# Doubling the token block of the two feed-forward phases to 512, with one SBUF buffer for the gate and the down weights

## The chip, the cores and the metric

One Trainium2 chip, 8 NeuronCores. Each core runs the same program on one batch element of 8192 tokens; nothing is exchanged between cores. The metric is the device time of the slowest core, in microseconds (us).

## The reference

```python
def ffn(x):                       # x [8, 8192, 1024], weights int32 in -127..127, scale 1/127
    gate = x @ (w_gate/127).T     # [.., 3072]
    up   = x @ (w_up/127).T       # [.., 3072]
    return (silu(gate) * up) @ (w_down/127).T      # [.., 1024]
x = x + 0.5 * ffn(layernorm(x))
x = x + causal_conv(layernorm(x), t)   # FFT over the sequence, filter t of 4096 steps
x = x + 0.5 * ffn(layernorm(x))
```

## The kernel before

All activations are kept transposed, with the 1024 channels as 8 chunks of 128 partitions and the tokens along the free dimension. The program has five stages in a row: the transform of the filter (`p0b`, with the weights cast to bf16 in DRAM beside it), the transposes of the weights (`p0a`), the first feed-forward phase (`ffn_phase("f1")`), the convolution (`p2`), and the second feed-forward phase (`ffn_phase("f3")`). Tiles of the two feed-forward phases carry `f1` or `f3` ahead of their names.

A feed-forward phase first loads the three weight matrices from DRAM into SBUF, each 128 partitions x 24576 bf16 (6144 KB), as `wgT` (gate), `wuT` (up) and `wdT` (down), through the DMA queue of SyncE (SP). They stay there for the whole phase. Then it goes over the tokens in `NBLK` blocks of `SB` = 256, that is 32 blocks. A block i has these steps:

- `prologue(i)`: GpSimd (POOL) issues the load of the block's input into `xsl`; ScalarE (ACT) squares all of it into `lnsl`; TensorE (PE) sums `xsl` and then the squares over the channels with a column of ones (L799 and L804, 8 matmuls each, into `pstat`); VectorE (DVE) makes the layernorm factors from the two rows of sums in about 24 operations on one partition (`rowmath`); SP stores them to DRAM.
- `prologue_b(i)`: POOL loads that row back, broadcast over the 128 partitions (`rbp`), and DVE multiplies it into `lnsl`, 8 operations.
- `gate_up(i)`: for each of the 24 hidden tiles `ht`, 8 gate matmuls (L864) and 8 up matmuls (L879), each with one extra matmul with a single row of weights (L860, L875) that subtracts the mean. ACT applies silu, DVE multiplies by the up result and writes `hid`.
- `down_store(i)`: for each of 8 output tiles, 24 matmuls from `hid` and `wdT` (L916), in PSUM banks that rotate over three; ACT evacuates into `res`, DVE adds the residual from `xsl`, and SP stores `res`. In f1 there follow the sums for the second layernorm (a square of `res` on ACT, L961 and L966 on PE, `row2` on DVE, two stores of a row by SP).

The order of the loop is `gate_up(i)`, `prologue(i+1)`, `prologue_b(i+1)`, `down_store(i)`. Every engine runs its own list strictly in this order; `rec.add` records an operation with the semaphores that it waits for. All ACT and DVE operations are recorded by one helper, so they have the line L83. The load of the next input waits only for its buffer (three `xsl` in f1, two in f3).

Of the kernel before, what the change touches and what calls it, by code (L numbers as in the profile page):

```python
# [6 lines left out]
F32 = mybir.dt.float32  # L7
BF16 = mybir.dt.bfloat16
# [4 lines left out]
SEQ, DIM, HID, KLEN = 8192, 1024, 3072, 4096  # L13
NFFT, P = 16384, 128
SCALE = float(np.float32(1.0 / 127.0))
EPS = 1e-5
SB = 256
NBLK = SEQ // SB
NCH = DIM // P
NHT = HID // P  # L20
# [151 lines left out]
class KB:  # L172
# [569 lines left out]
    def ffn_phase(self, tag):  # L742
        rec = self.rec
        self.mark()
        wgT = self.alloc(tag + "wgT", [P, NCH * HID], BF16)
        wuT = self.alloc(tag + "wuT", [P, NCH * HID], BF16)
        wdT = self.alloc(tag + "wdT", [P, NHT * DIM], BF16)
        nxs = 3 if tag == "f1" else 2
        xsl = [self.alloc(tag + f"xsl{i}", [P, NCH * SB], BF16) for i in range(nxs)]
        lnsl = [self.alloc(tag + f"lnsl{i}", [P, NCH * SB], BF16) for i in (0, 1)]  # L750
        hid = self.alloc(tag + "hid", [P, NHT * SB], BF16)
# [4 lines left out]
        res = self.alloc(tag + "res", [P, NCH * SB], BF16 if tag == "f1" else F32)  # L756
        T = lambda s: tag + s
        f1 = tag == "f1"

        bw = self.barrier_waits()  # L760
        for k, dst in (("g", wgT), ("u", wuT), ("d", wdT)):
            rec.add("sync", lambda sy, k=k, dst=dst: sy.dma_start(
                out=dst[:, :], in_=self.s_wT[k][:, :]),
                waits=[("wThbm", 48)] + bw, incs=[(T("wld" + k), 16)])

        pstat = self.pbank[0]
        pg = [self.pbank[2], self.pbank[3]]
        pu = [self.pbank[4], self.pbank[5]]
        pdn = [self.pbank[6], self.pbf.bitcast(F32), self.pbank[1]]
        xin = (self.xT if f1 else self.s_x2).rearrange("(c p) s -> p c s", p=P)  # L770

        def prologue(i):
            bi = i % 2
            xs = i % nxs
            lw = [("wsumev", 12 if "p0a" in self.phases else 0)]
            if i == 0:
                lw += bw
            if i >= nxs:
                lw.append((T("x1ev"), 8 * (i - nxs + 1)))
            if not f1:  # L780
                lw.append(("x2out", 16 * NGRP if "p2" in self.phases else 0))
            rec.add("gpsimd", lambda gg, i=i, xs=xs: gg.dma_start(
                out=xsl[xs].rearrange("p (c s) -> p c s", c=NCH),
                in_=xin[:, :, i * SB:(i + 1) * SB]),
                waits=[w for w in lw if w[1] > 0], incs=[(T("xld%d" % xs), 16)])
            sqw = [(T("xld%d" % xs), 16 * (i // nxs + 1)), (T("std"), rec.n(T("std")))]
            if i >= 2:
                sqw.append((T("umm"), rec.n(T("umm")) - NHT))
                if f1:
                    sqw.append((T("l2mm"), rec.n(T("l2mm"))))  # L790
            rec.add("scalar", lambda s, bi=bi, xs=xs: s.activation(
                lnsl[bi][:, :], xsl[xs][:, :], AF.Square),
                waits=sqw, incs=[(T("sqd"), 1)])
            stw = [(T("xld%d" % xs), 16 * (i // nxs + 1)), (T("row"), rec.n(T("row"))),
                   ("cst", 32), (T("l2row"), rec.n(T("l2row")))]
            if "p0a" in self.phases:
                stw.append(("wsumev", 12))
            for c in range(NCH):
                rec.add("tensor", lambda t, xs=xs, c=c: t.matmul(  # L799
                    pstat[0:1, 0:SB], self.misc[:, 0:1], xsl[xs][:, c * SB:(c + 1) * SB],  # L800
                    start=(c == 0), stop=(c == NCH - 1)),
                    waits=stw if c == 0 else [])
            for c in range(NCH):
                rec.add("tensor", lambda t, bi=bi, c=c: t.matmul(  # L804
                    pstat[0:1, SB:2 * SB], self.misc[:, 0:1], lnsl[bi][:, c * SB:(c + 1) * SB],
                    start=(c == 0), stop=(c == NCH - 1)),
                    waits=[(T("sqd"), rec.n(T("sqd")))] if c == 0 else [],
                    incs=[(T("std"), 1)] if c == NCH - 1 else ())
            def rowmath(v):
                s_, vv, y, tmp = (rows[0:1, k * SB:(k + 1) * SB] for k in range(4))  # L810
                v.tensor_copy(s_, pstat[0:1, 0:SB])
                v.tensor_mul(tmp, s_, s_)
                v.scalar_tensor_tensor(vv, tmp, -1.0 / DIM, pstat[0:1, SB:2 * SB],
                                       ALU.mult, ALU.add)
                v.tensor_scalar(vv, vv, 1.0, DIM * EPS, ALU.mult, ALU.add)
                v.tensor_single_scalar(y.bitcast(I32), vv.bitcast(I32), 1, ALU.logical_shift_right)
                v.tensor_scalar(y.bitcast(I32), y.bitcast(I32), -1, MAGIC, ALU.mult, ALU.add)
                for _ in range(4):
                    v.tensor_mul(tmp, y, y)
                    v.tensor_mul(tmp, tmp, vv)  # L820
                    v.tensor_scalar(tmp, tmp, -0.5, 1.5, ALU.mult, ALU.add)
                    v.tensor_mul(y, y, tmp)
                v.tensor_scalar(rows_bf[0:1, 0:SB], y, float(np.sqrt(DIM)), None, ALU.mult)
                return v.scalar_tensor_tensor(rows_bf[0:1, SB:2 * SB], s_,
                                              -1.0 / float(np.sqrt(DIM)), y,
                                              ALU.mult, ALU.mult)
            rmw = [(T("std"), rec.n(T("std")))]
            if f1:
                rmw.append(("l2out", rec.n("l2out")))
                if "ln2rows" in self.dbg:  # L830
                    rmw.append(("dbgout", rec.n("dbgout")))
            rec.add("vector", rowmath, waits=rmw, incs=[(T("row"), 1)])
            rec.add("sync", lambda sy, i=i: sy.dma_start(
                out=self.s_rb[tag][i % 2:i % 2 + 1, :], in_=rows_bf[0:1, 0:SB]),
                waits=[(T("row"), rec.n(T("row"))), (T("rbro"), rec.n(T("rbro")) - 16)
                       if rec.n(T("rbro")) >= 32 else (T("row"), rec.n(T("row")))],
                incs=[(T("rbro"), 16)])
# [13 lines left out]
        def gate_up(i):  # L851
            bi = i % 2
            for ht in range(NHT):
                q = ht % 2
                gw = [(T("lnap"), rec.n(T("lnap"))), (T("wldg"), 16)]
                if rec.n(T("silu")) >= 2:
                    gw.append((T("silu"), rec.n(T("silu")) - 1))
                for c in range(NCH):
                    if c == NCH - 1:
# [8 lines left out]
                        waits=gw if c == 0 else [],  # L868
                        incs=[(T("gmm"), 1)] if c == NCH - 1 else ())
# [3 lines left out]
                for c in range(NCH):  # L873
                    if c == NCH - 1:
# [8 lines left out]
                        waits=uw if c == 0 else [],  # L883
# [8 lines left out]
                if i > 0 and ht == 0:  # L892
                    hw.append((T("dmm"), rec.n(T("dmm"))))
                rec.add("vector", lambda v, ht=ht, q=q: v.tensor_mul(
                    hid[:, ht * SB:(ht + 1) * SB], silu[:, q * SB:(q + 1) * SB], pu[q][:, 0:SB]),
                    waits=hw, incs=[(T("hmul"), 1)])

        def down_store(i):
            bi = i % 2
            xs = i % nxs  # L900
            hm = rec.n(T("hmul"))
            for dt in range(NCH):
                pd = pdn[dt % 3]
                dw = []
                if dt == 0:
                    dw = [(T("hmul"), hm), (T("wldd"), 16)]
                    if i > 0:
                        dw.append((("x1out" if f1 else "o_out"), 16 * i))
                    if f1:
                        dw.append((T("l2row"), rec.n(T("l2row"))))  # L910
                    if "x1" in self.dbg and f1:
                        dw.append(("dbgout", rec.n("dbgout")))
                if dt >= 3:
                    dw.append((T("sdev"), rec.n(T("sdev")) - 2))
                for hc in range(NHT):
                    rec.add("tensor", lambda t, dt=dt, hc=hc, pd=pd: t.matmul(  # L916
                        pd[:, 0:SB] if True else None,
# [11 lines left out]
                    xsl[xs][:, dt * SB:(dt + 1) * SB]),  # L929
                    waits=[(T("sdev"), rec.n(T("sdev")))],  # L930
                    incs=[(T("x1ev"), 1)])
            if f1:
                x1o = self.s_x1.rearrange("(c p) s -> p c s", p=P)
                rec.add("sync", lambda sy, i=i: sy.dma_start(
# [17 lines left out]
            if f1:  # L952
# [11 lines left out]
                        waits=l2w0 if c == 0 else [])  # L964
                for c in range(NCH):
                    rec.add("tensor", lambda t, bi=bi, c=c: t.matmul(  # L966
                        pstat[0:1, SB:2 * SB], self.misc[:, 0:1],
                        lnsl[bi][:, c * SB:(c + 1) * SB], start=(c == 0), stop=(c == NCH - 1)),
                        waits=[(T("l2sq"), rec.n(T("l2sq")))] if c == 0 else [],
                        incs=[(T("l2mm"), 1)] if c == NCH - 1 else ())  # L970
                def row2(v):
# [2 lines left out]
                    b2 = rows[0:1, 5 * SB:6 * SB]  # L974
                    v.tensor_copy(s_, pstat[0:1, 0:SB])
                    v.tensor_mul(tmp, s_, s_)
                    v.scalar_tensor_tensor(vv, tmp, -1.0 / DIM, pstat[0:1, SB:2 * SB],
                                           ALU.mult, ALU.add)
                    v.tensor_scalar(vv, vv, 1.0, DIM * EPS, ALU.mult, ALU.add)
                    v.tensor_single_scalar(y.bitcast(I32), vv.bitcast(I32), 1, ALU.logical_shift_right)  # L980
# [95 lines left out]
```

How the kernel before makes its waits and increments, by code:

```python
            def wrapped(*a, **kw):  # L80
                if self._k > 0:
                    self._e.wait_ge(self._sem, self._k)
                ins = attr(*a, **kw)
                ins.then_inc(self._sem, 1)
                self._k += 1
                return ins
# [7 lines left out]
        def then_inc(self, *a, **k):  # L94
            return self
# [49 lines left out]
    def emit(self, eng_obj, name, sems, chain_sems):  # L145
        raw = eng_obj._e if isinstance(eng_obj, ChainedEngine) else eng_obj
        for wl, fn, il, nops in self.ops[name]:
            for s, v in wl:
                if v <= 0:
                    continue
                if s in self.owner:
                    need = {}
                    for vv in range(v, 0, -1):
                        e, c = self.mile[(s, vv)]
                        if e not in need:
                            need[e] = c
                        if len(need) == len(self.owner[s]):
                            break
                    for e, c in need.items():
                        raw.wait_ge(chain_sems[e], c)
                else:
                    raw.wait_ge(sems[s], v)
            k0 = eng_obj._k if isinstance(eng_obj, ChainedEngine) else 0
            ins = fn(eng_obj)
            if isinstance(eng_obj, ChainedEngine):
                assert eng_obj._k - k0 == nops, (name, nops, eng_obj._k - k0)
            for s, k in il:
                assert ins is not None
                ins = ins.then_inc(sems[s], k)
```

## Time and profile before

| | us |
|---|---|
| median of the 2 runs | 9327.43 (9175.94 to 9478.91) |
| the profiled execution | 9250.11 |
| its span, core 0, the slowest | 9248.6 |
| the other cores | 9120.6 to 9209.7 |
| first feed-forward phase, first gate matmul to last down matmul, core 0 | about 3074 |
| second feed-forward phase, the same, core 0 | about 2667 |

Times in the rows below are microseconds from the span's start unless a number is marked ns. PE is the matmul side of TensorE, PEld its weight load. A bracket at a row's end is the idle time of the engine before it and what ended it.

### The profile page before, as it was taken

The numbers are of one execution on the slowest core, as the hardware profiler recorded it, in microseconds if no ns is written. First come the engines' busy times: TensorE is split into PE (matmuls) and PEld (weight loads), VectorE is DVE, ScalarE is ACT, GpSimd is POOL, SyncE is SP. The second block draws the span as 40 slices with busy tenths as digits, with TensorE's granted clock in tenths as the row PEclk, the third lists the DMA queues.
The fourth block names the chain that finished last, engine by engine and source line by source line (L and its number), as shares of the span: only waits on it lengthen the run. The fifth ranks groups of instructions, "written<-read, shape, count | busy, mean of one in ns | idle before, by whom it ended". The sixth has DMA issues, their size and how long they took to land.

```text
span 9248.6 us, 186110 instructions; the slowest of 8 cores (9120.6 to 9248.6 us)
## 1 busy us (share of the span) xinstructions
PE 7401.4 (80%) x63384; PEld 5441.4 (59%) x63384; DVE 3739.8 (40%) x7613; ACT 2373.1 (26%) x3809; POOL 121.3 (1%) x165
## 2 busy tenths in 40 slices
PE   2555369898998989985666767676799999999999
PEld 1333246666666666664555656665577776777766
DVE  2555123333333333332666666676233332233322
ACT  2555111111111111111544443344111111111111
POOL 0000000000000000000000000000000000000000
PEclk9566679999999999997655556655799999999988
DMA  6421620000000000002011001101200000000000
GB/s 105 94 50 47 182 92 16 11 11 16 11 16 11 11 16 11 16 11 54 27 38 38 31 31 38 38 15 38 104 23 23 23 16 22 23 23 23 16 22 18
DMA packets 264327, 325.01 MB, mean 35 GB/s; under 512 B 116512, under 2 KB 215200, under 8 KB 259296
## 3 DMA queue, kind: packets, MB, share of 16 engines
q1 hardware_dynamic: 182288, 226.62, 7.3%
q0 software_dynamic: 81168, 86.49, 6.2%
q8 instruction: 582, 9.54, 0.4%
q14 instruction: 289, 2.37, 0.1%
HBM read 239.93 MB, written 138.51 MB: 41 GB/s over the span
## 4 chain that ended last, share of the span: by engine, by line
PE 58%; DVE 20%; DMA 6%; ACT 6%; issue 5%; another core or an unknown queue 3%; DVEq 1%; SPq 1%; ACTq 0%; POOL 0%; POOLq 0%
PE pb L864 16%; PE pb L879 16%; DVE f1rows L83 6%; PE pb L916 6%; DVE t_B L83 4%; DVE p2B L83 4%; PE pb L860 3%; PE pbf L916 3%; PE pb L875 3%; ACT p2win L83 2%; PE pb L634 2%; PE pb L639 2%; PE pb L602 2%; DMA s_that<-t_thim 2%
## 5 line engine op out<-in xcount | busy, mean ns | idle before, releaser
L879 PE MATMUL pb<-f1lnsl,f1wuT 128*128 128x256 bf16 x6144 | 988.0, 286 | 163.3 <-DVE f1hid L83 163.3
L864 PE MATMUL pb<-f1lnsl,f1wgT 128*128 128x256 bf16 x6144 | 988.1, 286 | 20.0 <-DVE f1lnsl L83 20.0
L864 PE MATMUL pb<-f3lnsl,f3wgT 128*128 128x256 bf16 x6144 | 957.0, 280 | 29.2 <-DVE f3lnsl L83 29.2
L879 PE MATMUL pb<-f3lnsl,f3wuT 128*128 128x256 bf16 x6144 | 956.6, 280 | 0.0
L83 DVE TENSOR_TENSOR f3hid<-f3silu,pb 128x256 bf16<-128x256 bf16 x768 | 323.4, 421 | 1499.7 <-PE pb L879 1497.0
L83 DVE TENSOR_TENSOR f1hid<-f1silu,pb 128x256 bf16<-128x256 bf16 x768 | 323.7, 421 | 1460.8 <-PE pb L879 1454.2
L879 PEld LDWEIGHTS pb<-f1lnsl,f1wuT 128*128 128x128 bf16 x6144 | 619.8, 101 | 339.5 <-issue 180.6
L83 ACT ACTIVATE f1silu<-pb 128x256 bf16<-128x256 f32 x768 | 294.9, 384 | 1890.2 <-PE pb L864 1548.3
L864 PEld LDWEIGHTS pb<-f1lnsl,f1wgT 128*128 128x128 bf16 x6144 | 619.6, 101 | 202.8 <-issue 43.7
L864 PEld LDWEIGHTS pb<-f3lnsl,f3wgT 128*128 128x128 bf16 x6144 | 609.3, 99 | 187.8 <-issue 29.9
L83 ACT ACTIVATE f3silu<-pb 128x256 bf16<-128x256 f32 x768 | 295.0, 384 | 1585.9 <-PE pb L864 1552.2
L879 PEld LDWEIGHTS pb<-f3lnsl,f3wuT 128*128 128x128 bf16 x6144 | 609.2, 99 | 157.4
L83 ACT CAST p2B<-pb 128x512 bf16<-128x512 f32 (+1 forms) x512 | 549.4, 1073 | 502.8 <-PE pb L608 465.7
L83 DVE CAST p2B<-pb 128x512 bf16<-128x512 f32 (+1 forms) x512 | 578.1, 1129 | 184.6 <-PE pb L608 145.2
L413 PE MATMUL pb<-f1sb,t_win 32*64 32x130 bf16 x2048 | 239.7, 334 | 424.3 <-DMA t_win<-t 252.0
L83 DVE CAST t_B<-pb 128x260 bf16<-128x260 f32 x256 | 397.5, 1553 | 260.4 <-PE pb L413 234.1
L634 PE MATMUL pb<-hhsb,p2B 128*64 128x64 bf16 x2048 | 452.8, 295 | 17.9 <-ACT p2B L83 17.9
L413 PEld LDWEIGHTS pb<-f1sb,t_win 32*64 32x64 bf16 x2048 | 165.3, 190 | 498.4 <-issue 475.3
L639 PE MATMUL pb<-hhsb,p2B 128*64 128x64 bf16 x2048 | 452.9, 295 | 0.0
L916 PE MATMUL pb<-f3hid,f3wdT 128*128 128x256 bf16 x3840 | 450.9, 279 | 1.0 <-DVE f3hid L83 1.0
L916 PE MATMUL pb<-f1hid,f1wdT 128*128 128x256 bf16 x3840 | 435.2, 273 | 1.1 <-DVE f1hid L83 1.1
L83 ACT CAST t_B<-pb 128x260 bf16<-128x260 f32 x256 | 394.9, 1543 | 148.3 <-PE pb L413 126.2
(122 smaller groups left out, 9865.8 us busy)
## 6 DMA issues: line engine op xcount, KB each, us to landing
out<-f3res SPq DMA_DIRECT2D x32, 1024.0 KB, 5.4
s_that<-t_thre SPq DMA_DIRECT2D x64, 256.0 KB, 2.0
s_that<-t_thim SPq DMA_DIRECT2D x64, 256.0 KB, 2.6
f1xsl<-xT POOLq DMA_DIRECT2D x32, 512.0 KB, 6.6
s_x<-f1res SPq DMA_DIRECT2D x32, 512.0 KB, 3.2
x1sl<-s_x SPq DMA_DIRECT2D x8, 2048.0 KB, 7.8
thre<-s_that SPq DMA_DIRECT2D x64, 256.0 KB, 2.7
thim<-s_that SPq DMA_DIRECT2D x64, 256.0 KB, 3.0
```

The costliest lines, as they stand in the source:

```text
L83: ins = attr(*a, **kw)
L413: rec.add("tensor", lambda t, ch=ch, ci=ci, l=l, pbank=pbank: t.matmul(pbank[64 * l:64 * l + 64, ci * 256:ci * 256 + 130], winv[64 * l:64 ...
L602: rec.add("tensor", lambda t, ch=ch, ci=ci, hi=hi, pbank=pbank: t.matmul(pbank[64 * hi:64 * hi + 64, ci * 256:(ci + 1) * 256], yre_v[64 * ...
L634: rec.add("tensor", lambda t, n1=n1, nq=nq, hh=hh, pb=pb: t.matmul(pb[64 * hh:64 * hh + 64, nq * 64:(nq + 1) * 64], ccv[:, :, 0, n1], hv[: ...
L639: rec.add("tensor", lambda t, n1=n1, nq=nq, hh=hh, pb=pb: t.matmul(pb[64 * hh:64 * hh + 64, nq * 64:(nq + 1) * 64], ccv[:, :, 1, n1], hv[: ...
L860: rec.add("tensor", lambda t, ht=ht, q=q: t.matmul(pg[q][:, 0:SB], self.gsum[0:1, ht * P:(ht + 1) * P], rows_bf[0:1, SB:2 * SB], start=Fal ...
L864: rec.add("tensor", lambda t, bi=bi, c=c, ht=ht, q=q: t.matmul(pg[q][:, 0:SB], wgT[:, c * HID + ht * P:c * HID + (ht + 1) * P], lnsl[bi][: ...
L875: rec.add("tensor", lambda t, ht=ht, q=q: t.matmul(pu[q][:, 0:SB], self.usum[0:1, ht * P:(ht + 1) * P], rows_bf[0:1, SB:2 * SB], start=Fal ...
L879: rec.add("tensor", lambda t, bi=bi, c=c, ht=ht, q=q: t.matmul(pu[q][:, 0:SB], wuT[:, c * HID + ht * P:c * HID + (ht + 1) * P], lnsl[bi][: ...
L916: rec.add("tensor", lambda t, dt=dt, hc=hc, pd=pd: t.matmul(pd[:, 0:SB] if True else None, wdT[:, hc * DIM + dt * P:hc * DIM + (dt + 1) * ...
```

## The change

The block grows from 256 to 512 tokens, so that a phase has 16 blocks, and every matmul, activation and vector operation of a block works on twice the columns. Sums of x and of its squares no longer fit one PSUM bank and take two (`pstat`, `pstat2`); the down tiles rotate over two banks in place of three, and f1 has two input buffers in place of three.

To make room in SBUF, `wdT` has no buffer of its own. It is a view of `wgT`. In each block POOL loads the down weights over the gate weights when the block's last gate matmul is done, and SP loads the gate weights back when the last down matmul is done; the down matmuls and the next block's gate matmuls wait for these loads.

```diff
-SB = 256
+SB = 512
...
-        wdT = self.alloc(tag + "wdT", [P, NHT * DIM], BF16)
-        nxs = 3 if tag == "f1" else 2
+        nxs = 2
...
+        wdT = wgT[:, 0:NHT * DIM]
...
-        for k, dst in (("g", wgT), ("u", wuT), ("d", wdT)):
+        for k, dst in (("g", wgT), ("u", wuT)):
...
-        pdn = [self.pbank[6], self.pbf.bitcast(F32), self.pbank[1]]
+        pdn = [self.pbank[6], self.pbf.bitcast(F32)]
...
-                gw = [(T("lnap"), rec.n(T("lnap"))), (T("wldg"), 16)]
+                gw = [(T("lnap"), rec.n(T("lnap"))), (T("wldg"), 16 * (i + 1))]
...
+                if ht == NHT - 1:
+                    rec.add("gpsimd", lambda gg: gg.dma_start(
+                        out=wdT[:, :], in_=self.s_wT["d"][:, :]),
+                        waits=[(T("gmm"), rec.n(T("gmm"))), ("wThbm", 48)],
+                        incs=[(T("wldd"), 16)])
...
-                pd = pdn[dt % 3]
+                pd = pdn[dt % 2]
                 dw = []
                 if dt == 0:
-                    dw = [(T("hmul"), hm), (T("wldd"), 16)]
+                    dw = [(T("hmul"), hm), (T("wldd"), 16 * (i + 1))]
...
-                if dt >= 3:
-                    dw.append((T("sdev"), rec.n(T("sdev")) - 2))
+                if dt >= 2:
+                    dw.append((T("sdev"), rec.n(T("sdev")) - 1))
...
+            if i + 1 < NBLK:
+                rec.add("sync", lambda sy: sy.dma_start(
+                    out=wgT[:, 0:NCH * HID], in_=self.s_wT["g"][:, :]),
+                    waits=[(T("dmm"), rec.n(T("dmm")))], incs=[(T("wldg"), 16)])
```

On POOL, from the first to the third block of f1, this stood before. `f1rbp` is the broadcast row, `f1xsl` the input block.

```order
L782 DMA f1xsl_61<-xT 128x8x256 [waits chain_v,thout,s2t,s1t,nymmt,ccst,wTdone,winldt,chain_s]
L841 DMA f1rbp<-s_rb_f 128x256 [waits f1rbro]
L782 DMA f1xsl_62<-xT 128x8x256 [waits chain_v]
L841 DMA f1rbp<-s_rb_f 128x256 [waits f1rbro,chain_v]
L782 DMA f1xsl_63<-xT 128x8x256 [waits chain_v]
```

And this stands there now. `f1gmm` counts finished groups of gate matmuls; the load of the down weights is shown with the name of the buffer, `f1wgT`.

```order
L783 DMA f1xsl_60<-xT 128x8x512 [waits chain_v,thout,s2t,s1t,nymmt,ccst,wTdone,winldt,chain_s]
L842 DMA f1rbp<-s_rb_f 128x512 [waits f1rbro]
L899 DMA f1wgT<-s_wdT 128x24576 [waits f1gmm,wThbm]
L783 DMA f1xsl_61<-xT 128x8x512 [waits chain_v]
L842 DMA f1rbp<-s_rb_f 128x512 [waits f1rbro,chain_v]
L899 DMA f1wgT<-s_wdT 128x24576 [waits f1gmm,wThbm]
```

The load of the next block's input now stands behind the load of the down weights, so it is issued only when the block's gate matmuls are done. On SP, after a block's down matmuls, there stood before:

```order
L833 DMA s_rb_f<-f1rowsbf 1x256 [waits chain_v,f1rbro]
L934 DMA s_x<-f1res 128x8x256 [waits chain_v,x1out]
L993 DMA s_ln<-f1rows 1x256 [waits chain_v,l2out]
L997 DMA s_ln<-f1rows 1x256
```

and now, with `f1dmm` counting finished groups of down matmuls:

```order
L834 DMA s_rb_f<-f1rowsbf 1x512 [waits chain_v,f1rbro]
L939 DMA f1wgT<-s_wgT 128x24576 [waits f1dmm]
L944 DMA s_x<-f1res 128x8x512 [waits chain_v,x1out]
L1003 DMA s_ln<-f1rows 1x512 [waits chain_v,l2out]
L1007 DMA s_ln<-f1rows 1x512
```

The reload of the gate weights stands ahead of the store of the block's result.

## Rows read from the trace of the kernel before

**Rows 1.** The page: PE's share, and its granted clock in 40 slices.
```profile
PE 7401.4 (80%) x63384; PEld 5441.4 (59%) x63384; DVE 3739.8 (40%) x7613; ACT 2373.1 (26%) x3809; POOL 121.3 (1%) x165
...
PEclk9566679999999999997655556655799999999988
```

**Rows 2.** Windows over the two feed-forward phases, core 0: start and end, length, busy times.
```profile
core 0: us, PE busy (x) PEld busy (x) DVE busy (x) ACT busy (x) POOL busy (x), PEclk, DMA share, GB/s
1235.00:4317.00 3082.00, 2792.22 (x20976) 1945.77 (x20976) 1023.63 (x2773) 513.52 (x1087) 44.47 (x61) 0.93 0.07 12
6577.00:9240.00 2663.00, 2645.49 (x20445) 1883.81 (x20444) 778.31 (x2015) 452.18 (x1054) 44.07 (x61) 0.96 0.07 20
```

**Rows 3.** Chain that ended last: a repeated point of f1, 30 periods apart, and of f3.
```profile
1310.99 3.15 DMA f1rbp<-s_rb_f
...
4205.45 3.13 DMA f1rbp<-s_rb_f
...
7539.49 5.24 PE pb L916 x48
7620.26 5.24 PE pb L916 x48
```

**Rows 4.** Timeline of f3, gate and up groups: start, length, engine, line.
```profile
7630.33 0.93 PE L864 MATMUL pb<-f3lnsl,f3wgT 128*128 128x256 bf16 x7
...
7631.52 0.93 PE L879 MATMUL pb<-f3lnsl,f3wuT 128*128 128x256 bf16 x7
...
7632.71 0.93 PE L864 MATMUL pb<-f3lnsl,f3wgT 128*128 128x256 bf16 x7
```

**Rows 5.** Timeline of f3, from the last up group to the down matmuls.
```profile
7603.96 1.91 ACT L83 ACTIVATE f3lnsl<-f3xsl 128x2048 bf16<-128x2048 bf16 x1
...
7604.40 1.03 PE L799 MATMUL pb<-f3xsl,misc 128*1 128x256 bf16 x8
...
7606.98 2.79 PE L916 MATMUL pb<-f3hid,f3wdT 128*128 128x256 bf16 x24
```

**Rows 6.** Loads of weights and input as f3 begins: issues, time to landing (last number), first use.
```profile
6519.54 0.32 SPq L762 DMA_DIRECT2D f3wgT<-s_wgT  x1
6521.81 0.32 SPq L762 DMA_DIRECT2D f3wuT<-s_wuT  x1
...
6520.29 0.94 POOL L782 DMA_DIRECT2D f3xsl<-s_x  x1 [2131.97 <-issue]
...
6543.13 1.87 PE L799 MATMUL pb<-f3xsl,misc 128*1 128x256 bf16 x8 [33.56 <-DMA f3xsl<-s_x]
...
s_wgT<-wtmp SPq DMA_DIRECT2D x1, 6144.0 KB, 18.6
...
f3wgT<-s_wgT SPq DMA_DIRECT2D x1, 6144.0 KB, 19.8
f3wuT<-s_wuT SPq DMA_DIRECT2D x1, 6144.0 KB, 32.3
```

**Rows 7.** DMA issues of core 4: the load of the gate weights in f3.
```profile
f3wgT<-s_wgT SPq DMA_DIRECT2D x1, 6144.0 KB, 26.1
```

**Rows 8.** Timeline of POOL in f1: the input load two blocks ahead.
```profile
2565.92 0.91 POOL L782 DMA_DIRECT2D f1xsl<-xT  x1
```

**Rows 9.** Timeline of f1's beginning: gate and up groups after 20 us without work.
```profile
1235.28 1.65 PE L864 MATMUL pb<-f1lnsl,f1wgT 128*128 128x256 bf16 x7 [20.00 <-DVE f1lnsl L83]
...
1237.37 1.70 PE L879 MATMUL pb<-f1lnsl,f1wuT 128*128 128x256 bf16 x7
...
1241.47 0.93 PE L879 MATMUL pb<-f1lnsl,f1wuT 128*128 128x256 bf16 x7
```

**Rows 10.** Timeline of f1 after a block's down matmuls: square, row of factors, next product.
```profile
2479.43 1.91 ACT L83 ACTIVATE f1lnsl<-f1res 128x2048 bf16<-128x2048 bf16 x1 [1.74 <-DVE f1res L83]
...
2483.59 0.41 DVE L83 COPY f1rows<-pb 1x256 f32<-1x256 f32 x1 [4.42 <-PE pb L966]
...
2495.53 1.65 PE L879 MATMUL pb<-f1lnsl,f1wuT 128*128 128x256 bf16 x7 [4.43 <-DVE f1hid L83]
```

More of the change, by code:

```diff
@@ L766, in ffn_phase @@
         pstat = self.pbank[0]
+        pstat2 = self.pbank[1]
         pg = [self.pbank[2], self.pbank[3]]
         pu = [self.pbank[4], self.pbank[5]]
-        pdn = [self.pbank[6], self.pbf.bitcast(F32), self.pbank[1]]
+        pdn = [self.pbank[6], self.pbf.bitcast(F32)]
         xin = (self.xT if f1 else self.s_x2).rearrange("(c p) s -> p c s", p=P)
@@ L804, in prologue @@
                 rec.add("tensor", lambda t, bi=bi, c=c: t.matmul(
-                    pstat[0:1, SB:2 * SB], self.misc[:, 0:1], lnsl[bi][:, c * SB:(c + 1) * SB],
+                    pstat2[0:1, 0:SB], self.misc[:, 0:1], lnsl[bi][:, c * SB:(c + 1) * SB],
                     start=(c == 0), stop=(c == NCH - 1)),
@@ L812, in rowmath @@
                 v.tensor_mul(tmp, s_, s_)
-                v.scalar_tensor_tensor(vv, tmp, -1.0 / DIM, pstat[0:1, SB:2 * SB],
+                v.scalar_tensor_tensor(vv, tmp, -1.0 / DIM, pstat2[0:1, 0:SB],
                                        ALU.mult, ALU.add)
@@ L966, in down_store @@
                     rec.add("tensor", lambda t, bi=bi, c=c: t.matmul(
-                        pstat[0:1, SB:2 * SB], self.misc[:, 0:1],
+                        pstat2[0:1, 0:SB], self.misc[:, 0:1],
                         lnsl[bi][:, c * SB:(c + 1) * SB], start=(c == 0), stop=(c == NCH - 1)),
@@ L976, in row2 @@
                     v.tensor_mul(tmp, s_, s_)
-                    v.scalar_tensor_tensor(vv, tmp, -1.0 / DIM, pstat[0:1, SB:2 * SB],
+                    v.scalar_tensor_tensor(vv, tmp, -1.0 / DIM, pstat2[0:1, 0:SB],
                                            ALU.mult, ALU.add)
```

## The prediction

> **What bounds the kernel now.** I read the page first, then windows over the two phases that the change touches, then the chain and the timeline of single blocks. TensorE is busy for 80% of the span [rows 1]; the busy shares of the other engines are small. In the feed-forward phases it is the bound almost alone: it works for 2792 of 3082 us in f1 and for 2645 of 2663 us in f3 [rows 2], with DMA at 7%. So f3 has nothing to hide a new wait behind, and f1 has some 290 us of idle time.
>
> The period of a block is (4205.45 - 1310.99)/30 = 96.5 us in f1 and 80.8 us in a stretch of f3 at full clock [rows 3]; over the phase f3 takes 2665/32 = 83.3 us, since core 0 has a granted clock of 0.96 there [rows 2]. A gate or up group (9 matmuls of 256 columns) starts 1.19 us after the one before it [rows 4], and a down matmul takes 5.24/48 = 0.109 us [rows 3]. That makes f3's block: 48 x 1.19 = 57.1, down 192 x 0.109 = 20.9, and 2.6 us for the sums, from the L799 matmuls to the first down matmul [rows 5]; together 80.6. In f1 the second layernorm adds about 16 us: the sums wait for a square of 1.91 us, and the row of factors keeps DVE from 2483.6 to 2495, so that PE waits 4.43 us for a product [rows 10], and it comes back at half clock.
>
> **The change part by part, for a block of 512.**
>
> Matmuls. 256 more columns at 2.4 GHz are 0.107 us, nearly the whole of a down matmul's 0.109; the rest of a gate group is 1.19 - 9 x 0.107 = 0.23 us that belongs to no column. It comes once per group and I take it as fixed: 1.19 + 9 x 0.107 = 2.15 us in place of 2.38. The upper bound is 2.38 (all of it doubles). Gate and up: 48 x 2.15 = 103.2 against 114.2, a gain of 11.0. Down: 192 x 0.216 = 41.5 against 41.9, a gain of 0.4. This is all that PE can gain, (11.0 + 0.4) x 32 blocks = 365 us over both phases.
>
> Load of the down weights. It is issued when the last gate group is done, and only the last up group, 2.15 us, covers it. A load of this size landed 19.8 us after its issue with an input load on the other queue beside it, the next one behind it 14.8 us later, and a store of the same bytes alone took 18.6 [rows 6]. Bounds: 14.8 below, and 26.1 above, what core 4 needed [rows 7]. I take 18.6, the transfer that ran alone. Issued by POOL instead of SP it moves the same rows; I add 1 us for POOL's two issues of 0.9 us, which go out one behind the other [rows 6].
>
> What stands behind it. Before, the input of block i+1 was issued most of a block ahead (at 2565.92, ninety microseconds before its use) [rows 8] and cost nothing. Now it is queued on POOL behind the down weights' load, its 1 MB (f3, bf16) or 2 MB (f1, f32) comes after 6.3 MB in the same queue, and at 6.3 MB in 14.8 us it adds 2.4 us in f3 and 4.9 us in f1. So the input lands 22.0 us (f3) and 24.5 us (f1) after the last gate group. PE runs in order: the sums of block i+1 stand ahead of the down matmuls. They need the square on ACT, 1.91 us for 2048 columns [rows 5], about 3.7 for 4096, and then 8 matmuls at half clock after the pause, 1.87 us for 256 columns [rows 6], about 3.6 for 512. That is 7.4 us more with the handovers. From the end of the last up group to the first down matmul: 22.0 + 7.4 - 2.15 = 27.2 us in f3 and 29.8 in f1, against 2 x 2.6 = 5.2 now [rows 5].
>
> Reload of the gate weights. It is issued after the last down matmul, and the next block's first gate matmul waits: 18.6 plus 0.4 for the handover, 19.0 us, with the same bounds. In f3 nothing is left for PE in that time. In f1 the second layernorm's square, sums and row lie under it: 1.5 us for the last evacuation and addition, 3.7 square, 3.6 sums, 16 to 17 us for the row (11.4 us in rows 10, with 0.27 or 0.13 us more per operation of the 24) end near 26 us, about when the first product is due (19.0 + 2 groups at half clock), so this cover costs nothing. The store of the result, now behind the reload on SP, is only waited for by the next down matmuls.
>
> Clock. After 20 us without work, three groups took 6.2 us until the engine ran at 2.4 GHz again, against 3.57 [rows 9]: 2.6 us lost at each return to the gate matmuls. At the return after the input wait the sums, already priced at half clock, take the loss. [...]
>
> The rest. Two PSUM banks for the down tiles: an evacuation by ACT (well below 1.9 us, which 2048 columns take [rows 5]) against 5.2 us of matmuls, nothing. The factor row and the 8 multiplications on DVE, some 28 us, lie under 41.5 us of down matmuls. One weight load less at a phase's start saves 14.8 us, but the first input, square, sums and row are longer by as much: nothing. Longer tails of the two phases: +12 us.
>
> **The sum.** f3: 103.2 + 27.2 + 41.5 + 19.0 + 2.6 = 193.5; 16 blocks without the last reload are 3096 - 22 = 3074 us against 2665 now, +409. f1: 103.2 + 29.8 + 41.5 + 19.0 + 2.6 = 196.1; 3138 - 22 = 3116 against 32 x 96.5 = 3087, +29. With the tails 9250 + 409 + 29 + 12 = 9700. There are 62 loads of 6.3 MB now, and some will meet those of another core; 20 us for that (an estimate from rows 7, a few loads at the longer time) gives 9720 us, 5.1% over the profiled execution of 9250. That run lies 77 us below the median of the two runs, which are 3% apart, so I hold to the profiled one. A measurement of this kernel can tell about 2% from no change.
>
> **The rivals.**
>
> Crowded memory. Core 4 needed 26.1 us where core 0 needed 19.8 [rows 6, 7]. If all 62 loads take that long, 62 x 7.5 = 465 us come on top: 10,165; if half do, 9930. For it: before, the loads came once; now all cores repeat them every 195 us. Against it: a core loads for about a fifth of the time. In the Trainium skill (DMA: Bandwidth & Descriptors, Measured) a core has some 358 GB/s when its neighbour streams too, and 436 at most; by that a load would take 17.6 us of transfer in place of 14.4, and the sum would be at most 200 us higher. It is weighed in this rival's chance.
>
> The input is not late (this one ends on the other side, not slower). If the DMA engines work on the input beside the down weights and not behind them, square and sums are done under the load: 7.3 us less per block, 234 us. If besides the loads take 14.8 us and not 18.6, 62 x 3.8 = 236 go too: 9720 - 470 = 9250, no change. It decides once the stall before the down matmuls is below 18 us and the reload below 15. For it: the second load landed 14.8 us after the first. Against it: in f3 the input, issued 0.8 us after the gate weights, was there only at 6543.1, after they had landed [rows 6].
>
> Matmuls of 512 columns overlap. If the time from one matmul to the next grew by much less than the columns, PE would gain far more. From rows: if a matmul of 512 columns cost 0.13 us in place of 0.216, 624 a block x 0.085 x 32 = 1700 us: 8020. Against it: 0.109 us for 256 columns is their number at 2.4 GHz, and at half clock the group nearly doubled [rows 9], so columns are the price. The Trainium skill (TensorE: Matmul & The Clock Gate, Back-to-back issue gap) gives 131 ns for 512 columns in a sustained stream, beside 216 for a single pair; the trace bears out the second kind of count.
>
> **How the numbers follow.** The forecast has 0.74, the crowded memory 0.15, the early input 0.08, the overlap 0.03. The time is the likeliest case's, 9720. Its own bounds are 9480 (all loads at 14.8) and, with gate groups that gain only half of their 0.23 us (1536 groups x 0.115 = 177 us) and some contention, 10,050, which takes in half of the crowded case. So the range is 9480 to 10,050. Faster 0.03 (the overlap), within 2% 0.09 (the early input and the edge of the forecast), slower 0.88.
>
> **What would show it.** In the profile after: gate groups 2.15 us apart; a wait of PE of about 20 us for the input, ended by the DMA of `f1xsl` and `f3xsl`, ahead of L800; a wait of 19 us ahead of the first gate matmuls (in f1 shorter by the sums in it), ended by the DMA of `f1wgT` and `f3wgT`; loads landing in 18 to 20 us; periods of 196 and 193 us; f3 longer by some 400 us and f1 by little. It is wrong if f1 loses as much as f3, if gate groups stay at 2.38 us, if loads take 25 us or more, or if PE's wait ahead of the sums is short.

## The result and the profile after

The changed kernel is slower, by 5.3%: the ratio to the kernel before is 1.0526, with a 95% interval of 1.0489 to 1.0563. The medians of all runs are 9900 and 9290 us; they hold executions in which the cores of one die ran at a lower granted clock, which the ratio leaves out. The profiled execution took 9655 us, 405 more than the one of before. A span given alone below is that of one profiled execution. The kernel before, run again beside the experiments, took 9169 to 9226 us at its shortest, so the difference between the spans of two kernels is good to some 50 us, unless a ratio is given.

The page of the kernel after, against [rows 1]: a third fewer matmuls, TensorE busy 72% in place of 80%, and DMA is now second in the chain that ended last.

```profile
span 9653.8 us, 129035 instructions; the slowest of 8 cores (9589.8 to 9653.8 us)
...
PE 6906.3 (72%) x42648; PEld 3505.7 (36%) x42648; DVE 3367.6 (35%) x5181; ACT 2183.7 (23%) x2737; POOL 91.3 (1%) x133
...
PE 59%; DMA 18%; DVE 13%; issue 3%; ACT 3%; another core or an unknown queue 2%; SPq 1%; DVEq 0%; ACTq 0%; POOL 0%; POOLq 0%
```

Waits of TensorE, longest first, of the feed-forward phases: total, times, longest. The first line of each phase is the wait for the next block's input in the middle of a block, the second that for the gate weights at its end. The longest 99.5 us of the first line is the phase's start, before the loop.

```profile
PE pb L800 <- DMA f1xsl<-xT: 429.9, 16, 99.5
PE pb L800 <- DMA f3xsl<-s_x: 340.7, 16, 45.2
...
PE pb L865 <- DMA f3wgT<-s_wgT: 289.4, 15, 19.7
...
PE pb L865 <- DMA f1wgT<-s_wgT: 177.3, 15, 12.3
```

The loads of the same kernel: queue, count, size, time from issue to landing. The medians are near the 18.6 to 19.8 us of [rows 6], and none is at the 26 us of [rows 7]. Of all 496 loads in the loops of the eight cores the longest took 20.5 us.

```profile
f1wgT<-s_wgT SPq DMA_DIRECT2D x16, 6144.0 KB, 18.7
f1wgT<-s_wdT POOLq DMA_DIRECT2D x16, 6144.0 KB, 17.8
f3wgT<-s_wgT SPq DMA_DIRECT2D x16, 6144.0 KB, 19.0
f3wgT<-s_wdT POOLq DMA_DIRECT2D x16, 6144.0 KB, 17.8
...
f1xsl<-xT POOLq DMA_DIRECT2D x16, 1024.0 KB, 22.4
...
f3xsl<-s_x POOLq DMA_DIRECT2D x16, 1024.0 KB, 20.1
```

The timeline of one block of f3, which answers to [rows 4, 5 and 9]: start, length, engine, line. GpSimd issues the down weights and right behind them the input; the square and the sums start 20.7 us later; the first down matmul (L922) starts 25.8 us after the last up group ended, 20.0 of wait and 5.8 of sums. Then the reload: 19.06 us idle, the first seven matmuls at half clock (3.05 us in place of 1.67, the group 3.53 us in all), and from there groups 2.15 us apart.

```profile
7856.36 0.53 POOL L899 DMA_DIRECT2D f3wgT<-s_wdT  x1 [144.88 <-PE pb L865]
7856.99 0.90 POOL L783 DMA_DIRECT2D f3xsl<-s_x  x1
...
7877.69 3.62 ACT L83 ACTIVATE f3lnsl<-f3xsl 128x4096 bf16<-128x4096 bf16 x1 [21.13 <-DMA f3xsl<-s_x]
...
7877.90 3.57 PE L800 MATMUL pb<-f3xsl,misc 128*1 128x512 bf16 x8 [20.00 <-DMA f3xsl<-s_x]
...
7881.45 2.31 PE L805 MATMUL pb<-f3lnsl,misc 128*1 128x512 bf16 x8
...
7883.70 5.35 PE L922 MATMUL pb<-f3hid,f3wgT 128*128 128x512 bf16 x24
...
7944.37 3.05 PE L865 MATMUL pb<-f3lnsl,f3wgT 128*128 128x512 bf16 x7 [19.06 <-DMA f3wgT<-s_wgT]
...
7947.90 1.67 PE L880 MATMUL pb<-f3lnsl,f3wuT 128*128 128x512 bf16 x7
...
7950.05 1.67 PE L865 MATMUL pb<-f3lnsl,f3wgT 128*128 128x512 bf16 x7
```

The period of a block follows from the chain, where the reload's start comes back once a block, 14 blocks apart here: (4128.95 - 1415.46)/14 = 193.8 us in f1, (9458.96 - 6774.79)/14 = 191.7 us in f3.

```profile
1415.46 18.55 DMA f1wgT<-s_wgT
...
4128.95 19.16 DMA f1wgT<-s_wgT
...
6774.79 19.18 DMA f3wgT<-s_wgT
...
9458.96 18.69 DMA f3wgT<-s_wgT
```

From its first gate matmul to its last down matmul f1 took 3073 us (3071 before by the trace, not the 3074 of the table ahead) and f3 3042 us (2666 before), each on the slowest core of its execution. So f3 carries 376 of the 405 us and f1 2; the later starts of the two phases add 5 and 19, the end 3.

The 2666 us are not f3 at full clock. In that execution cores 0 and 1 ran f3 at a mean granted clock of 0.96 and took 2666 and 2665 us; the other six had 0.99 to 1.00 and took 2586 to 2588. Core 5, for one:

```profile
6577.00:9240.00 2663.00, 2539.17 (x20276) 1836.42 (x20273) 775.28 (x2006) 447.55 (x1045) 43.98 (x61) 1.00 0.07 21
```

Against those six cores f3 lost some 450 us (3032 to 3042 us on the eight cores after).

### The profile page after: what moved, and what is told of

The parts are those of the page before. It is cut to its first block, busy times and chain, and to the rows that moved or that the text cites. A ratio compares the mean times of both kernels' runs of the same rounds, so it can differ in the third digit from the quotient of the medians.

```text
span 9653.8 us, 129035 instructions; the slowest of 8 cores (9589.8 to 9653.8 us)
## 1 busy us (share of the span) xinstructions
PE 6906.3 (72%) x42648; PEld 3505.7 (36%) x42648; DVE 3367.6 (35%) x5181; ACT 2183.7 (23%) x2737; POOL 91.3 (1%) x133
## 4 chain that ended last, share of the span: by engine, by line
PE 59%; DMA 18%; DVE 13%; issue 3%; ACT 3%; another core or an unknown queue 2%; SPq 1%; DVEq 0%; ACTq 0%; POOL 0%; POOLq 0%
PE pb L865 15%; PE pb L880 14%; PE pb L922 7%; PE pbf L922 7%; DVE p2B L83 4%; DMA f1xsl<-xT 4%; DVE t_B L83 4%; DMA f3xsl<-s_x 3%; DMA f3wgT<-s_wgT 3%; DMA f1wgT<-s_wgT 3%; PE pb L861 3%; PE pb L876 2%; ACT p2win L83 2%; PE pb L634 2%; PE pb L639 2%
## 5 line engine op out<-in xcount | busy, mean ns | idle before, releaser
L865 PE MATMUL pb<-f3lnsl,f3wgT 128*128 128x512 bf16 x3072 | 816.8, 390 | 315.9 <-DMA f3wgT<-s_wgT 289.4
L865 PE MATMUL pb<-f1lnsl,f1wgT 128*128 128x512 bf16 x3072 | 817.3, 390 | 203.7 <-DMA f1wgT<-s_wgT 177.3
L880 PE MATMUL pb<-f1lnsl,f1wuT 128*128 128x512 bf16 x3072 | 797.6, 382 | 0.0
L880 PE MATMUL pb<-f3lnsl,f3wuT 128*128 128x512 bf16 x3072 | 796.8, 382 | 0.0
L865 PEld LDWEIGHTS pb<-f3lnsl,f3wgT 128*128 128x128 bf16 x3072 | 302.8, 99 | 694.8 <-issue 434.0
L865 PEld LDWEIGHTS pb<-f1lnsl,f1wgT 128*128 128x128 bf16 x3072 | 302.6, 99 | 583.6 <-issue 322.8
L880 PEld LDWEIGHTS pb<-f1lnsl,f1wuT 128*128 128x128 bf16 x3072 | 301.2, 98 | 364.4 <-issue 96.5
L880 PEld LDWEIGHTS pb<-f3lnsl,f3wuT 128*128 128x128 bf16 x3072 | 301.0, 98 | 363.5 <-issue 95.0
L634 PEld LDWEIGHTS pb<-hhsb,p2B 128*64 128x64 bf16 x2048 | 416.2, 203 | 21.0 <-issue 21.0
L639 PEld LDWEIGHTS pb<-hhsb,p2B 128*64 128x64 bf16 x2048 | 416.2, 203 | 0.0
L602 PE MATMUL pb<-winvsb,yhre 64*64 64x256 bf16 x2048 | 306.6, 322 | 113.1 <-DVE yhim L83 104.7
## 6 DMA issues: line engine op xcount, KB each, us to landing
f1wgT<-s_wdT POOLq DMA_DIRECT2D x16, 6144.0 KB, 17.8
f3wgT<-s_wdT POOLq DMA_DIRECT2D x16, 6144.0 KB, 17.8
```

What stands on the lines that cost most here:

```text
L602: rec.add("tensor", lambda t, ch=ch, ci=ci, hi=hi, pbank=pbank: t.matmul(pbank[64 * hi:64 * hi + 64, ci * 256:(ci + 1) * 256], yre_v[64 * ...
L634: rec.add("tensor", lambda t, n1=n1, nq=nq, hh=hh, pb=pb: t.matmul(pb[64 * hh:64 * hh + 64, nq * 64:(nq + 1) * 64], ccv[:, :, 0, n1], hv[: ...
L639: rec.add("tensor", lambda t, n1=n1, nq=nq, hh=hh, pb=pb: t.matmul(pb[64 * hh:64 * hh + 64, nq * 64:(nq + 1) * 64], ccv[:, :, 1, n1], hv[: ...
L865: rec.add("tensor", lambda t, bi=bi, c=c, ht=ht, q=q: t.matmul(pg[q][:, 0:SB], wgT[:, c * HID + ht * P:c * HID + (ht + 1) * P], lnsl[bi][: ...
L880: rec.add("tensor", lambda t, bi=bi, c=c, ht=ht, q=q: t.matmul(pu[q][:, 0:SB], wuT[:, c * HID + ht * P:c * HID + (ht + 1) * P], lnsl[bi][: ...
```

## The experiments

### Both loads in the loop left out

```diff
-                if ht == NHT - 1:
-                    rec.add("gpsimd", lambda gg: gg.dma_start(
-                        out=wdT[:, :], in_=self.s_wT["d"][:, :]),
...
-            if i + 1 < NBLK:
-                rec.add("sync", lambda sy: sy.dma_start(
-                    out=wgT[:, 0:NCH * HID], in_=self.s_wT["g"][:, :]),
...
```

> Left out: both loads in the loop, of the down weights over the gate weights and back, so the down product is made with the gate weights. All work of the 512-token block stays. Theory (the waits for the reloads are the whole loss, the wider matmuls gain): a block of f3 is 103.2 (gate, up) + about 6 (sums) + 41.5 (down) = 151 us, 16 of them 2410 against 3085 in the changed kernel; in f1 the row of factors of the second layernorm (16.6 us on one partition of VectorE) is no longer under a wait and costs TensorE some 15 us, about 170 us a block, 2720 against 3075. In sum about 8620 us, some 630 below the kernel before. Rival 1 (the 512-token block has costs of its own, the two PSUM banks for the down tiles or the longer operations on VectorE): above 9000. Rival 2 (without pauses the granted clock falls as in the last part of f3 before): between 8700 and 8850.

Measured: a ratio of 0.9335 (0.9308 to 0.9362) to the kernel before, the lowest time 8562 us. On core 0, f3 took 2386 us and f1 2633 us. The first rival falls: 2386/16 = 149.1 us a block is what the matmuls need, 103.2 + 41.5 and 4.3 for the sums. The second falls with the two executions of 8562 and 8569 us; on core 0 f3 had a granted clock of 1.00. What I had too high is the wait for the second layernorm's row in f1, now without a cover: 7 us a block on core 0, where I wrote 15.

```profile
PE pb L880 <- DVE f1hid L83: 104.8, 15, 7.3
```

The second layernorm as a whole costs more than that wait. A block of f1 is (2633 - 2386)/16 = 15.4 us longer than one of f3: beside the wait there are its sums, the short waits ahead of them, and a start at half clock behind it. For 256 tokens it was 15.7 us (96.5 - 80.8, [rows 3]), and it comes once a block, half as often with blocks of 512.

So the larger block alone is worth 6.6%, the loads cost more than that. That is some 600 us, against the 365 of the prediction's "all that PE can gain", which counted the matmuls alone: on core 0 f1 became 438 us shorter, and f3 some 200 against the cores at full clock.

### The reload of the gate weights left out

```diff
-            if i + 1 < NBLK:
-                rec.add("sync", lambda sy: sy.dma_start(
-                    out=wgT[:, 0:NCH * HID], in_=self.s_wT["g"][:, :]),
-                    waits=[(T("dmm"), rec.n(T("dmm")))], incs=[(T("wldg"), 16)])
```

> Left out: the reload of the gate weights after the down product; the gate product uses the down weights from the second block on. The load of the down weights stays, with the input behind it. Theory: in f3 the 19.1 us wait and the start at half clock go, 20 us a block or 300 us in all; in f1 only 12 us of wait are there to be had, and of these some 10 come back as a wait for the second layernorm's row of factors, so 2 to 5 us a block, 30 to 75 us. About 9300 us. Rival (the cover in f1 is not needed and the whole load is saved in both): 9655 - 30 x 20 = 9055.

Measured: a span of 9259.4 us, 394 below the changed kernel's. The theory holds, the rival (9055) falls: f3 became 317 us shorter and f1 75, the upper edge of what was written. In f1 more than half of the saved wait of 177 us comes back, as the same wait of 104.8 us in all for the product as in the run before:

```profile
PE pb L880 <- DVE f1hid L83: 104.8, 15, 7.3
```

### Half of each load

```diff
-                        out=wdT[:, :], in_=self.s_wT["d"][:, :]),
+                        out=wdT[:, 0:NHT * DIM // 2], in_=self.s_wT["d"][:, 0:NHT * DIM // 2]),
...
-                    out=wgT[:, 0:NCH * HID], in_=self.s_wT["g"][:, :]),
+                    out=wgT[:, 0:NCH * HID // 2], in_=self.s_wT["g"][:, 0:NCH * HID // 2]),
```

> The changed kernel, with both loads in the loop cut to half their columns (3 MB each); left out is the other half, so gate and down products use mixed weights. Theory (the waits are transfer time): 3.15 MB less at 14.5 to 15 us per 6.3 MB, so each load lands 7.3 us earlier, in 10.5 to 11.5 us; in f3 both waits shrink by 7.3 us, 16 x 7.3 + 15 x 7.3 = 226 us; in f1 the wait for the input shrinks as much, 117 us, and the one for the gate weights from 12 to about 5 us, but with the row of factors then late for the first products by some 5 us, so 30 to 110 us. In all 370 to 450 us less, about 9240. Rival (a large part of each load is a fixed cost): loads of 14 us and more, 9400 or above.

Measured: a span of 9228.9 us, 425 less, as written. The rival, loads of 14 us and more, falls. The DMA issues:

```profile
f1wgT<-s_wdT POOLq DMA_DIRECT2D x16, 3072.0 KB, 10.2
f3wgT<-s_wdT POOLq DMA_DIRECT2D x16, 3072.0 KB, 10.4
f1wgT<-s_wgT SPq DMA_DIRECT2D x15, 3072.0 KB, 11.1
f3wgT<-s_wgT SPq DMA_DIRECT2D x15, 3072.0 KB, 11.2
```

Half the bytes land 7.4 to 7.8 us earlier than 17.8 to 19.0, so by this difference 14.8 to 15.6 us of a whole load grow with the bytes and about 3 do not. The waits are bytes over rate, 3.15 MB in 7.6 us being 414 GB/s, and those 3 us.

### The input issued ahead of the down weights

```diff
+        load_x(0)
         prologue(0)
         prologue_b(0)
         for i in range(NBLK):
+            if i + 1 < NBLK:
+                load_x(i + 1)
             gate_up(i)
```

`load_x` is the DMA that stood at the head of `prologue`.

> The changed kernel whole, with one thing moved: GpSimd issues the input of block i+1 ahead of the gate and up products of block i, so it stands in front of the load of the down weights and not behind it. Theory (the input, the square and the sums behind the down load are a third of the wait): from the last up matmul to the first down matmul 25.4 us become about 16.5 to 17 in f3 and 28.3 become the same in f1; the down matmuls then begin at half clock and lose up to 2.6 us of it. 16 x (6 to 9) + 16 x (9 to 12) = 240 to 330 us less, about 9370. Rival (the wait is the down weights' own, the input comes with them): within 60 us of 9655.

Measured: 1.0307 (1.0277 to 1.0337) of the kernel before, a span of 9450.7 us, 203 below the changed kernel's. The rival falls, but the gain is below the 240 to 330 us that were written. The timeline of f3 shows the sums (L803, L808) directly behind the up matmuls (7900.8), the wait shortened, and the down matmuls starting at 7917.19, 16.4 us after the sums began, as expected:

```profile
7900.78 1.89 PE L803 MATMUL pb<-f3xsl,misc 128*1 128x512 bf16 x8
7903.35 1.89 PE L808 MATMUL pb<-f3lnsl,misc 128*1 128x512 bf16 x8 [0.69 <-ACT f3lnsl L83]
7917.19 6.75 PE L925 MATMUL pb<-f3hid,f3wgT 128*128 128x512 bf16 x24 [11.95 <-DMA f3wgT<-s_wdT]
7923.77 1.46 PE L925 MATMUL pbf<-f3hid,f3wgT 128*128 128x512 bf16 x6
```

The first down tile takes 6.6 us (7917.19 to 7923.77) in place of 5.2: behind the pause the granted clock was 0.50 (7917.2 to 7919.9). The periods by the issues of the down load are 185.2 us in both phases, 8.6 less than in the changed kernel in f1 and 6.5 less in f3, about 240 us over 32 blocks. Over the 15 periods of each phase, f1 became 130 us shorter and f3 99. The span fell by 203 only: on the slowest core f1 begins 14 us later, 9 of them because the first loads took longer (the first input landed after 46 us in place of 38; that of the second block was issued only afterwards), and between the phases lie 11 us more. Why is open.

### The down weights issued by SyncE

```diff
-                    rec.add("gpsimd", lambda gg: gg.dma_start(
+                    rec.add("sync", lambda gg: gg.dma_start(
                         out=wdT[:, :], in_=self.s_wT["d"][:, :]),
```

> The changed kernel, with the load of the down weights issued by SyncE's queue instead of GpSimd's; GpSimd still issues the input of the next block when its turn comes, but with nothing in front of it, and its buffer is free since the block before, so the input is loaded during the gate and up products. Theory (it is the place behind the down load on GpSimd that makes the input late): the same as with the input issued ahead, 9450 us within 40. Rival (the down load is faster or slower from the other queue): its time to landing other than 17 to 19 us, and the sum other by 32 times the difference.

Measured: a span of 9470.6 us. The load lands in 17.1 to 17.4 us against 17.8, inside the 17 to 19 us beyond which the rival would begin, and the input is gone from TensorE's list of waits but for the phase's start; in its place stand the down weights, about 12 us at a time and 15.5 at most:

```profile
PE pb L922 <- DMA f3wgT<-s_wdT: 183.6, 16, 15.4
PE pb L865 <- DMA f1wgT<-s_wgT: 171.6, 15, 12.5
PE pb L922 <- DMA f1wgT<-s_wdT: 130.1, 11, 15.5
```

So two edits that have only the order on GpSimd in common give the same 180 to 200 us. It was the place behind the down load that made the input late.

### The shared buffer with blocks of 256

```diff
-        wdT = self.alloc(tag + "wdT", [P, NHT * DIM], BF16)
...
+        wdT = wgT[:, 0:NHT * DIM]
...
-        for k, dst in (("g", wgT), ("u", wuT), ("d", wdT)):
+        for k, dst in (("g", wgT), ("u", wuT)):
```

and the two loads of the change, in each of 32 blocks.

> The kernel before, blocks of 256, with the shared buffer alone: the down weights loaded over the gate weights and back in each of the 32 blocks. Theory (the price hangs on the number of loads, and the larger block only halves it): per block of 256 in f3 about 22 us more between up and down, 19 of reload and 2.6 of clock, 44 us x 32 = 1400; in f1 about 24 + 6 + 1 = 31 us x 32 = 1000. About 11,600 us. Rival (the loads get shorter when asked for twice as often, or lie under each other): below 10,700; rival (the memory gets crowded): above 12,200, with loads of 22 us and more.

Measured: a span of 11453.4 us. Two points of the chain in f3, one block apart:

```profile
8029.75 20.11 DMA f3xsl<-s_x
...
8154.73 21.06 DMA f3xsl<-s_x
```

The period is 125.0 us where [rows 3] have 80.8: 44 us a block, as written. With 126 loads in place of 62 the medians of their landing times are 18.0 to 18.9 us, and the longest of any core's in the loops 22.0. The price hangs on the number of loads, and their medians do not rise when all eight cores ask twice as often. The whole came out 150 us, 1.3%, below the expectation.

### A full block of weights for the extra matmul, in the kernel before and in the changed one

Each gate and up group has one matmul with a single row of weights. Here it has 128 rows, of which 127 are zero; the result is the same.

```diff
-        self.gsum = self.alloc("gsum", [1, HID], BF16)
-        self.usum = self.alloc("usum", [1, HID], BF16)
+        self.gsum = self.alloc("gsum", [P, HID], BF16)
+        self.usum = self.alloc("usum", [P, HID], BF16)
...
+        rec.add("vector", lambda v: v.memset(self.gsum[:, :], 0.0), incs=[("cst1", 1)])
+        rec.add("vector", lambda v: v.memset(self.usum[:, :], 0.0), incs=[("cst1", 1)])
...
-                            pg[q][:, 0:SB], self.gsum[0:1, ht * P:(ht + 1) * P],
-                            rows_bf[0:1, SB:2 * SB], start=False, stop=False,
+                            pg[q][:, 0:SB], self.gsum[:, ht * P:(ht + 1) * P],
+                            rows_bf[:, SB:2 * SB], start=False, stop=False,
```

(and the same for `usum`; `rows_bf` has 128 rows as well and is cleared once a phase.) In the kernel before:

> The kernel before with one thing else: the extra matmul of each gate and up group has 128 rows of weights, 127 of them zero, in place of a single row; what is computed is the same. Theory (the 0.23 us per group that belong to no column come from the single-row matmul, whose weights and those of the matmul after it are not loaded under a running matmul): a group takes 9 x 0.109 = 0.98 us in place of 1.19, and 3072 groups x 0.21 = 645 us go: about 8610 us. Rival (the 0.23 us come with every change of accumulation group or PSUM bank): groups stay at 1.19 us, 9250 us. Rival (the granted clock falls when TensorE has no such breaks): groups near 1.0 to 1.1 us, 8700 to 9000.

In the changed kernel:

> The changed kernel with the same edit, 128 rows for the extra matmul. Theory (the gain of the 512-token block is that this cost per group comes half as often, so without the cost nothing is left of it): a group takes 9 x 0.216 = 1.94 us in place of 2.15, 1536 groups x 0.21 = 320 us less, about 9335 us, so the distance to the kernel before with the same edit grows from 5% to over 8%. Rival (512-column groups hide the weight loads anyhow): groups stay at 2.15, 9655 us.

Measured in the kernel before: 0.9371 (0.919 to 0.955) of the time, a span of 8590.8 us, the fastest whole kernel of this study. The interval is wide because it rests on three executions of each, but they lie far apart: 8592, 8592 and 8703 us against 9193, 9213 and 9278. The timeline of f3:

```profile
6952.82 0.93 PE L867 MATMUL pb<-f3lnsl,f3wgT 128*128 128x256 bf16 x7
6953.58 0.27 PE L863 MATMUL pb<-f3rowsbf,gsum 128*128 128x256 bf16 x1
6953.69 0.27 PE L867 MATMUL pb<-f3lnsl,f3wgT 128*128 128x256 bf16 x1
6953.80 0.93 PE L882 MATMUL pb<-f3lnsl,f3wuT 128*128 128x256 bf16 x7
```

A group takes 0.98 us in place of 1.19, and the extra matmul and its neighbour follow 0.11 us apart. The mean granted clock of f3 was 1.00 on all eight cores of this execution, and the last ten slices of the page's row have 0.9 and more; that rival falls as well.

```profile
PEclk9566659999999999998555665556689999999999
```

In the changed kernel the span is 9371.7 us, 282 less than without the edit where 320 were written, and groups take 1.94 us:

```profile
7060.71 1.67 PE L883 MATMUL pb<-f3lnsl,f3wuT 128*128 128x512 bf16 x7
7062.22 0.38 PE L879 MATMUL pb<-f3rowsbf,usum 128*128 128x512 bf16 x1
7062.44 0.38 PE L883 MATMUL pb<-f3lnsl,f3wuT 128*128 128x512 bf16 x1
7062.65 1.67 PE L868 MATMUL pb<-f3lnsl,f3wgT 128*128 128x512 bf16 x7
```

With the edit in both, the 512-token kernel lies 9371.7/8590.8 = 9.1% above the 256-token one. Two groups of 256 take 1.96 us, one of 512 takes 1.94: wider matmuls gain next to nothing once the single row is gone. Of the 0.23 us per group that belong to no column, 0.21 are the price of that row, at 256 columns (1.19 - 0.98) and at 512 (2.15 - 1.94).

## Why the prediction was right

The forecast was 9720 us for a profiled time of 9250, 5.1% more. The measured ratio is 1.0526, and the profiled execution of the changed kernel took 9655, so the sum was 65 us too high. That 5.1% and 5.3% agree still better than the times is luck. The forecast started from an execution of 9250 us that had f3 at a granted clock of 0.96 on its slowest core, while its block after was added up at full clock. The five shortest of the other executions before took 9172 to 9205 us: from there 9720 is 5.6 to 6%, and from 9250 the measured 9655 is 4.4%. The two slips cancel in the percentage. The mechanism stands on its own feet, term by term:

- Matmuls. Groups of 2.15 us were forecast and stand in the timeline of the changed kernel. Rival "matmuls of 512 columns overlap" is refuted: a down tile of 24 takes 5.18 us, 0.216 us a matmul, and the 0.13 us that it was priced at stands in no row. The "sustained stream" figure of the Trainium skill (TensorE: Matmul & The Clock Gate, Back-to-back issue gap), 131 ns for 512 columns, is not what this stream of weight loads and matmuls shows; its figure of some 216 ns, which it gives for isolated matmuls, is.
- Down weights and input. 27.2 us from the last up to the first down matmul were forecast for f3 and 25.8 measured in the block shown (median 25.6); in f1 29.8 forecast and a median of 27.6. The wait itself is right in f3 (20.0 us before the sums; 22.0 - 2.15 = 19.9 forecast). The 1.4 us too much are in the square and the sums, 5.8 us in f3 where I had 7.4: the second row of sums was no longer at half clock all through (2.31 us for 8 matmuls, against 3.57 for the first 8).
- Reload of the gate weights. 19.0 us forecast, 19.06 measured in the block of f3 shown and 19.3 on the average. In f1 the second layernorm is fully covered by it, as said: the row of factors was ready before the first product, and no wait for it appears.
- Clock at the return. 2.6 us forecast from [rows 9], one return of the kernel before. In the block shown the first group took 3.53 in place of 2.15 us, 1.4 us lost. Over the returns of the slowest core, from the start of a block's first group to that of its seventh, the loss runs from 1.3 to 2.9 us with a mean of 2.0, so 2.6 was near the top.
- Periods: 196.1 and 193.5 us forecast, 193.8 and 191.7 measured. Over 16 blocks that is 37 and 29 us too much.
- Tails and meetings in memory. I had 12 and 20 us. The later starts and the end came to 27 us. Of the 20 us for loads that meet, nothing is seen in the landing times, 17.3 to 20.5 us on all eight cores, and the rival "crowded memory" is refuted by them and again with 126 loads.
- "The input is not late" is refuted by the waits of the changed kernel, and the two runs that took the input out of its place show what it would have been worth: 180 to 200 us, where I wrote 234.

Added up against the slowest cores: f3 409 us forecast and 376 measured, f1 29 and 2, the meetings 20 and nothing, the tails 12 and 27. That is 33 + 27 + 20 - 15 = 65 us, the distance from 9720 to 9655.

One reading behind the prediction was incomplete: I took the 0.23 us as a cost per group that only larger blocks can thin out. The runs with the full block of weights show that nearly all of it can be removed, at no cost in memory to speak of, and for about the gain that the larger block brought without its loads (6.3% and 6.6%).

## What to carry to other kernels

Sharing one buffer between two weights that are used in turn makes their loads serial with TensorE, and the price is bytes over rate per round; compare it with what the freed memory buys before looking at anything else. When a wait is added to an in-order queue, list what stands behind it: here over a third of the time between up and down matmuls (25.8 us against 16.4) was not the weights but the input and the sums queued after them. A small constant cost per group is worth a look at its rows before one enlarges the group to thin it out.

## What was not expected of the hardware

A matmul with one row of weights costs twice, once ahead of itself and once ahead of the matmul behind it. In the kernel before, seven matmuls from 7630.33 on would end near 7631.09 at 0.109 us each; the extra one starts at 7631.19, and its neighbour 0.21 us later. Each is 0.10 us late. In the timeline each of the two weight loads begins with its own matmul and not under the one before (the first two rows are the extra matmul, the second two the one behind it):

```profile
7631.19 0.09 PEld L860 LDWEIGHTS pb<-f3rowsbf,gsum 1*128 1x128 bf16 x1 [0.21 <-issue]
7631.19 0.28 PE L860 MATMUL pb<-f3rowsbf,gsum 1*128 1x256 bf16 x1
...
7631.40 0.10 PEld L864 LDWEIGHTS pb<-f3lnsl,f3wgT 128*128 128x128 bf16 x1
7631.40 0.28 PE L864 MATMUL pb<-f3lnsl,f3wgT 128*128 128x256 bf16 x1
```

With 128 rows for all, both are hidden: in that run the same two loads start 0.11 us ahead of their matmuls (6953.47 and 6953.58 against 6953.58 and 6953.69). Why the loads are not taken ahead across a change in the number of rows is open; that 128 rows cure it is shown. At 512 columns the price is the same (behind the seven matmuls from 7950.05 on, which need 1.51 us, the extra one starts at 7951.65 and the next at 7951.97, 0.32 us apart where 0.216 would do).
